# A recommendation tower on one core: gathered rows copied aside by ScalarE, GpSimd's gathers split in two, and edits at the two ends

## The reference

```python
x = stack([tbl_f[ids[:, f]] for f in range(32)], axis=1)             # 1024 x 32 x 32
h = x
for i, (W, b) in enumerate([(W0, b0), (W1, b1), (W2, b2)]):          # 128, 128, 1 outputs
    z = einsum('bhd,bmd,ohm->bod', h, x, W.reshape(O, H, 32))
    z = relu(z + b)
    h, direct = (z[:, :half], z[:, half:]) if i < 2 else (None, z)   # half = 64
    directs.append(direct)
feat = concat([sum(concat(directs, 1), -1), dense_ctx], 1)           # 1024 x 145
y = relu(relu(feat @ W_top1 + b_top1) @ W_top2 + b_top2) @ W_top3    # 1024 x 1
```

## Time and profile before

| what | value |
|---|---|
| time, median of 3 runs | 1219.24 us (1217.71 to 1222.34) |
| profiled execution: time, span | 1219.3 us, 1217.3 us |
| busy: PE, DVE | 1120.3 us (92%), 1055.8 us (87%) |
| busy: POOL, ACT | 717.5 us (59%), 579.5 us (48%) |
| chain that ended last, by engine | DVE 36%, issue 23%, POOL 21%, PE 12%, DMA 5% |
| mean granted TensorE clock | 0.983 |
| transfers | 154.95 MB, mean 127 GB/s |

### The profile page before, as it was taken

How to read it: one execution, slowest core, us unless ns; L and a number is a source line. 1 busy time by engine, 2 the same in 40 slices (tenths; PEclk the granted TensorE clock), 3 DMA queues, 4 the chain that set the end, 5 groups by cost and what they waited for, 6 DMA issues and landing times.

```text
span 1217.3 us, 11479 instructions
## 1 busy us (share of the span) xinstructions
PE 1120.3 (92%) x3736; PEld 682.4 (56%) x3736; DVE 1055.8 (87%) x573; ACT 579.5 (48%) x477; POOL 717.5 (59%) x333
## 2 busy tenths in 40 slices
PE   0699989999999999999999999899999999999998
PEld 0356655655555555565565656556565555656655
DVE  1689987998898989899898989889899898999973
ACT  0344554554555445455444545545445554544534
POOL 6277665667766666766566686656676665663110
PEclk9899998999999999999999999999999999999999
DMA  7555553455454435555344555434554543354200
GB/s 231 175 156 156 130 137 105 117 134 155 136 146 107 137 94 155 141 143 148 107 128 109 155 138 145 134 103 119 136 155 129 148 125 110 112 152 126 54 1 0
DMA packets 63414, 154.95 MB, mean 127 GB/s; under 512 B 12753, under 2 KB 29394, under 8 KB 63394
## 3 DMA queue, kind: packets, MB, share of 16 engines
q1 hardware_dynamic: 52594, 147.05, 42.2%
q0 software_dynamic: 8192, 4.21, 2.4%
q10 hardware_dynamic: 2608, 3.44, 0.9%
HBM read 95.79 MB, written 8.39 MB: 86 GB/s over the span
## 4 chain that ended last, share of the span: by engine, by line
DVE 36%; issue 23%; POOL 21%; PE 12%; DMA 5%; SPq 1%; DVEq 1%; ACT 0%; POOLq 0%; ACTq 0%
POOL gathered L330 15%; DVE prod L476 12%; DVE raw L531 11%; PE z_ps L635 11%; DVE prod_lo L537 7%; POOL prod_lo L350 6%; DMA x_roll<-x_dram 3%; DVE raw L502 3%; DVE top_a L551 1%; DVE lo L509 1%; DVE h2x L544 1%; PE mlp_ps L635 1%; POOL prod_lo L341 1%; DMA x_base<-x_dram 1%; DMA gathered<-in_table,rows_sb 0%
## 5 line engine op out<-in xcount | busy, mean ns | idle before, releaser
L635 PE MATMUL z_ps<-prod,w_sb 128*128 128x512 f32 x1280 | 582.0, 599 | 49.9 <-DVE prod L489 27.5
L330 POOL DMA_INDIRECT gathered<-in_table,rows_sb x256 | 431.8, 1687 | 96.3 <-issue 72.2
L531 DVE TENSOR_TENSOR raw<-h_roll,x_roll 128x2048 f32<-128x2048 f32 x160 | 363.1, 2285 | 81.5 <-POOL prod_lo L350 80.2
L872 ACT CAST prod_hi<-raw 128x2048 fp32r<-128x2048 f32 x160 | 304.9, 1906 | 257.6 <-DVE raw L531 253.0
L635 PEld LDWEIGHTS z_ps<-prod,w_sb 128*128 128x128 f32 x1280 | 244.1, 192 | 318.5 <-issue 306.3
L341 POOL TENSOR_TENSOR prod_lo<-raw,prod_hi 128x2048 fp32r<-128x2048 f32 x32 | 146.7, 4585 | 335.4 <-DVE prod_lo L537 290.2
L476 DVE TENSOR_TENSOR prod<-mlp_ps,x_roll 128x2048 f32<-128x2048 f32 x124 | 281.0, 2284 | 17.1 <-DMA x_roll<-x_dram 6.8
L635 PE MATMUL z_ps<-prod_hi,w_hi 128*128 128x512 f32 x648 | 245.3, 459 | 43.5 <-POOL prod_lo L350 41.4
L537 DVE TENSOR_TENSOR prod_lo<-raw,prod_hi 128x2048 fp32r<-128x2048 f32 x98 | 223.6, 2283 | 0.0
L635 PE MATMUL z_ps<-prod_lo,w_hi 128*128 128x512 f32 x648 | 209.3, 404 | 0.0
L635 PE MATMUL z_ps<-prod_hi,w_lo 128*128 128x512 f32 x648 | 209.1, 403 | 0.0
(11 more groups left out here) (61 smaller groups left out, 371.6 us busy)
## 6 DMA issues: line engine op xcount, KB each, us to landing
x_roll<-x_dram SPq DMA_DIRECT2D x128, 512.0 KB, 4.8
x_base<-x_dram SPq DMA_DIRECT2D x32, 512.0 KB, 3.6
h_roll<-h_roll SPq DMA_DIRECT2D x32, 448.0 KB, 4.5
h_roll<-h_roll SPq DMA_DIRECT2D x32, 384.0 KB, 5.4
h_roll<-h_roll SPq DMA_DIRECT2D x32, 320.0 KB, 6.0
x_dram<-gathered SPq DMA_DIRECT2D x64, 128.0 KB, 1.7
h_roll<-h_roll SPq DMA_DIRECT2D x32, 192.0 KB, 7.2
gathered<-in_table,rows_sb POOLq DMA_INDIRECT x256
```

The lines of the kernel that those rows point to most:

```text
L330: nc.gpsimd.indirect_dma_start(gathered[:, u, g * DIM:(g + 1) * DIM], None, table, bass.IndirectOffsetOnAxis(ap=rows_sb[:, col:col + 1], a ...
L531: nc.vector.tensor_tensor(raw[:, RAW_SLOT[r], :, :], hs, xs, ALU.mult).then_inc(raw_ready, 1)
L635: return nc.tensor.matmul(*args, **kw)
L872: nc.scalar.copy(prod_hi[:, SPLIT_SLOT[r], :, :], raw[:, RAW_SLOT[r], :, :]).then_inc(hi_ready, 1)
```

## The change

1. **A copy aside.** ScalarE copies the gathered chunk c+1 into a new buffer `x_late` (2 buffers, 128x256) in step c, between the roundings of A1 and B2 (`copy_late`). `h2x` reads `x_late` in place of `gathered`. The gathers of chunk c+3 now wait for that copy of chunk c-1 (`late_copied`), which ran two steps earlier, and not for h2x.
2. **Gathers four and four.** GpSimd's order becomes lo3, (rows for the next four chunks where u is 1), four gathers, lo1, four gathers.
3. **Late load of an MLP weight.** `wt2_sb` has no buffer of its own: it lies in a part of `x_roll`, and is loaded by SyncE after the last roll of h, not at the start by ScalarE's queue. The room pays for `x_late`.
4. **Start.** TensorE runs 6 extra matmuls (128x512, float32) once x of chunk 0 is stored, and 3 after layer 0 of chunk 0; what they write to `z1_ps` is never read. SyncE loads `x_base` of chunk 1 before `x_part16` and the second half of `x_roll` of that chunk (it waits, as before, for the first two products), not behind them.
5. **Last chunk.** Its layer 1 accumulates in `z0_ps`, so it need not wait until ScalarE has drained `z1_ps` of chunk 30; TensorE runs `layer2_u` of chunk 30 after B0, not ahead of it. The MLP's banks are taken in the order z1, mlp, z0, with other waits to match.

The diff, cut to its core:

```diff
+        x_late = sb("x_late", [P, 2, PART])
...
+        wt2_sb = x_roll[:, 0, M2, :].rearrange("p (k n) -> p k n", n=TOP2)
...
-        mlp_banks = [t[:, k * BANK:(k + 1) * BANK] for t in (z0_ps, mlp_ps, z1_ps) for k in range(2)]
+        mlp_banks = [t[:, k * BANK:(k + 1) * BANK] for t in (z1_ps, mlp_ps, z0_ps) for k in range(2)]
+
+        def z1_of(c):
+
+            return z0_ps if is_last(c) else z1_ps
...
-                wait(pool, h2x_ready, freed)
-                for g in range(GATHERS):
+                wait(pool, late_copied, freed)
+                for g in range(part * GATHERS // 2, (part + 1) * GATHERS // 2):
...
-                lo1(c)
                 ahead = UNROLL - 1
-                if not isinstance(c, int) or c + ahead < CHUNKS:
+                more = not isinstance(c, int) or c + ahead < CHUNKS
+                if more:
                     if u == 1:
                         make_rows(group + 1)
-                    gather(c + ahead, (u + ahead) % UNROLL, group if u == 0 else group + 1)
+                    gather(c + ahead, (u + ahead) % UNROLL, group if u == 0 else group + 1, 0)
+                lo1(c)
+                if more:
+                    gather(c + ahead, (u + ahead) % UNROLL, group if u == 0 else group + 1, 1)
...
                     if b == 1:
+                        if isinstance(c, int) and c == 1:
+                            sp.wait_ge(prod_ready, PAIRS0)
+                            load_base(c)
...
-                if isinstance(c, int) and c == 1:
-                    sp.wait_ge(prod_ready, PAIRS0)
-                    load_base(c)
...
             roll_h(CHUNKS - 1, (CHUNKS - 1) % 2)
+            sp.wait_ge(raw_ready, (CHUNKS - 1) * SPLIT1)
+            sp.dma_start(wt2_sb, wt2).then_inc(mlp_loaded, 16)
...
                 dve.wait_ge(u_done, c + 1)
+                dve.wait_ge(late_copied, c + 1)
                 wait(dve, z2_done, group)
-                nc.vector.tensor_tensor(h2x[:, u, :], u_ps[:, :], gathered[:, u, :], ALU.mult).then_inc(h2x_ready, 1)
+                nc.vector.tensor_tensor(h2x[:, u, :], u_ps[:, :], x_late[:, u % 2, :], ALU.mult).then_inc(h2x_ready, 1)
...
+            def keep_clock(count):
+
+                for _ in range(count):
+                    mm(z1_ps[:, 0:BANK], w0_sb[:, 0, :], w0_sb[:, :, :].rearrange("p r n -> p (r n)"),
+                       start=True, stop=True)
 
             pe.wait_ge(w0_ready, 1)
+            pe.wait_ge(x_stored[0], 32)
+            keep_clock(6)
             for k in range(PAIRS0):
                 layer0(0, 0, k)
             pe.wait_ge(w16_ready, 1)
             layer0_pairs16(0)
+            keep_clock(3)
...
+            def copy_late(c, u, group):
+
+                act.wait_ge(gather_done[u], (group + 1) * (16 * GATHERS))
+                wait(act, h2x_ready, c - 1)
+                nc.scalar.copy(x_late[:, u % 2, :], gathered[:, u, :]).then_inc(late_copied, 1)
...
                 round_products(c, A1)
+                if not is_last(c):
+                    copy_late(c + 1, (u + 1) % UNROLL, group if u < UNROLL - 1 else group + 1)
                 round_products(c, B2)
```

More of the change, by code:

```diff
@@ L244, in build_tower @@
         lo1_ready = sem("lo1_ready")
+        late_copied = sem("late_copied")
         h0_copied = sem("h0_copied")
@@ L319, in make_rows, with gather @@
                                         ALU.add).then_inc(rows_made, 1)
-            def gather(c, u, group):
+            def gather(c, u, group, part):
                 made = settled(pool, group + 1)
@@ L358, in step @@
                     lo3(c - 1)
-                lo1(c)
                 ahead = UNROLL - 1
-                if not isinstance(c, int) or c + ahead < CHUNKS:
+                more = not isinstance(c, int) or c + ahead < CHUNKS
+                if more:
                     if u == 1:
                         make_rows(group + 1)
-                    gather(c + ahead, (u + ahead) % UNROLL, group if u == 0 else group + 1)
+                    gather(c + ahead, (u + ahead) % UNROLL, group if u == 0 else group + 1, 0)
+                lo1(c)
+                if more:
+                    gather(c + ahead, (u + ahead) % UNROLL, group if u == 0 else group + 1, 1)
             make_rows(0)
             for c in range(UNROLL - 1):
-                gather(c, c, 0)
+                for part in range(2):
+                    gather(c, c, 0, part)
             over_chunks(pool, step)
@@ L616, in _ @@
             dve.wait_ge(split_used, CHUNKS * SPLIT1)
-            nc.vector.tensor_copy(wt2_hi, wt2_sb[:, :, :]).then_inc(wt2_hi_ready, 1)
+            nc.vector.tensor_copy(wt2_hi, wt2_sb).then_inc(wt2_hi_ready, 1)
             dve.wait_ge(wt2_hi_ready, 1)
-            nc.vector.tensor_tensor(wt2_lo, wt2_sb[:, :, :], wt2_hi, ALU.subtract).then_inc(wt2_ready, 1)
+            nc.vector.tensor_tensor(wt2_lo, wt2_sb, wt2_hi, ALU.subtract).then_inc(wt2_ready, 1)
             for n in range(BATCH_HALVES * M1):
@@ L677, in layer1 @@
             def layer1(c, u, k):
-                whole(z1_ps, first1(c) + k, slot1(c, u) + k, w1_sb[:, k * PAIR:(k + 1) * PAIR, :], start=k == 0)
+                whole(z1_of(c), first1(c) + k, slot1(c, u) + k, w1_sb[:, k * PAIR:(k + 1) * PAIR, :], start=k == 0)
             def layer0_pairs16(c):
@@ L716, in step @@
                     layer0(*after, 1)
-                wait(pe, h2_ready, 2 * c)
-                wait(pe, direct1_ready, c)
+                if is_last(c):
+                    pe.wait_ge(h1_ready, 2 * CHUNKS)
+                    pe.wait_ge(direct0_ready, CHUNKS)
+                else:
+                    wait(pe, h2_ready, 2 * c)
+                    wait(pe, direct1_ready, c)
                 layer1(c, u, 0)
@@ L722, in step @@
                     layer0_pairs16(c + 1)
-                if not_first(c):
+                    if not_first(c):
+                        layer2_u(c - 1, (u - 1) % UNROLL)
+                split(z1_of(c), c, B0)
+                if is_last(c):
                     layer2_u(c - 1, (u - 1) % UNROLL)
-                split(z1_ps, c, B0)
                 layer1(c, u, 1)
-                split(z1_ps, c, B1)
+                split(z1_of(c), c, B1)
                 layer1(c, u, 2)
-                split(z1_ps, c, A1)
+                split(z1_of(c), c, A1)
                 if u == 0 and not_first(c):
                     layer2_sum(c, group - 1)
-                split(z1_ps, c, B2)
+                split(z1_of(c), c, B2)
                 if not pool_makes_lo3(c):
-                    split(z1_ps, c, B3, stop=True)
+                    split(z1_of(c), c, B3, stop=True)
+            def keep_clock(count):
+                for _ in range(count):
+                    mm(z1_ps[:, 0:BANK], w0_sb[:, 0, :], w0_sb[:, :, :].rearrange("p r n -> p (r n)"),
+                       start=True, stop=True)
             pe.wait_ge(w0_ready, 1)
+            pe.wait_ge(x_stored[0], 32)
+            keep_clock(6)
             for k in range(PAIRS0):
@@ L765, in _ @@
             pe.wait_ge(mlp_loaded, 16 * 7)
-            pe.wait_ge(direct0_ready, CHUNKS)
-            pe.wait_ge(h1_ready, 2 * CHUNKS)
+            pe.wait_ge(direct1_ready, CHUNKS - 1)
+            pe.wait_ge(h2_ready, 2 * (CHUNKS - 1))
+            pe.wait_ge(prod_ready, first1(CHUNKS - 1) + WHOLE1)
             pe.wait_ge(direct_summed, CHUNKS // BATCH_HALVES)
@@ L827, in _ @@
             act.dma_start(wt1b_sb[:, :], wt1b).then_inc(mlp_loaded, 16)
-            act.dma_start(wt2_sb[:, :, :], wt2).then_inc(mlp_loaded, 16)
             act.dma_start(wt3_sb[:, :], wt3).then_inc(mlp_loaded, 16)
@@ L855, in relu1 @@
                     nc.scalar.activation(h2[half * HID:(half + 1) * HID, s, :],
-                                         z1_ps[0:HID, half * BANK:(half + 1) * BANK], ACT.Relu,
+                                         z1_of(c)[0:HID, half * BANK:(half + 1) * BANK], ACT.Relu,
                                          bias=b1_sb[0:HID, :]).then_inc(h2_ready, 1)
-                nc.scalar.activation(direct[HID:P, s, :], z1_ps[HID:P, :], ACT.Relu,
+                nc.scalar.activation(direct[HID:P, s, :], z1_of(c)[HID:P, :], ACT.Relu,
                                      bias=b1_sb[HID:P, :]).then_inc(direct1_ready, 1)
@@ L920, in _ @@
             copy_h0(0, 0)
+            copy_late(0, 0, 0)
             over_chunks(act, step)
```

1 line of the change is left out of this document (removed).

## The result

| | before | after |
|---|---|---|
| median (range, runs) | 1218.47 us (1216.57 to 1222.34, 4) | 1134.82 us (1133.59 to 1136.96, 4) |
| ratio, 95% interval | | 0.9312 [0.9284, 0.9339] |
| profiled execution: time, span | 1219.3, 1217.3 us | 1133.59, 1131.7 us |
| PE, DVE busy | 92%, 87% | 97%, 90% |
| mean granted TensorE clock | 0.983 | 0.999 |

The account below looks back on a forecast made before the run. The prediction took VectorE's losses to late lo3 as the bound, TensorE being next. From 1219.3 us it took 68.3 (steady chunks), 3 (start) and 3 (last chunk), giving 1145 us; 8-in-10 range 1134 to 1180.

Parts of the forecast that it names:

- The bound: Steady chunks: VectorE loses time to late lo3, behind eight gathers; with lo3 on time TensorE bounds at 33.15 us a chunk.
- Where 123 us of VectorE's loss would go: Steady chunks: VectorE's 80.2 us waiting for lo3 and 43 us of stretched raw16 go; only the part above TensorE's pace returns.
- Lateness of lo1: Steady chunks: four gathers ahead of lo1 delay it; 0.25 us a chunk beyond VectorE's slack, making 33.4 us a chunk.
- the sign "idle ahead of lo1 falls under 2 us": GpSimd in steady chunks: lo1's idle time ahead of it was to fall from 9.5 us to under 2.
- The start: Start: earlier x_base load taken as 2 us, extra matmuls as 1; 3 us saved, from 0 to 6.
- The last chunk: Last chunk: first layer-1 product starts without the drain wait, at full clock; 3 us saved, from 1 to 5.
- The copy at nothing: ScalarE, each chunk: one copy of 0.40 us taken to cost 0; 11 us if wholly on the path.
- the late weight at nothing: Late load of wt2, some 35 us before it is needed: taken to cost 0.
- The inference of the Trainium skill: Gather descriptor writing not held up by a tensor_tensor; if so, lo1 never late and 33.15 us a chunk, 7 us less.
- (a): Steady chunks: VectorE stays the bound, gathers missing seams in most chunks; 1169 to 1210 us, middle 1178; chance 0.22.
- (b): Every steady chunk: lo1 3.8 us late into A1, lo3 2.1 us into raw16; 1264 us; chance 0.03.
- (c): Steady chunks: lo3 as late as before, its four gathers missing as often as eight; 1213 to 1219 us; chance 0.05.

Follow-up runs that it names:

- x9: Changed kernel, TensorE leaving out the rounded part times the weights' remainder in two of five split products (A1, B2); 1083.19 us, 0.8875 of the kernel before.
- x10: Changed kernel, TensorE leaving out the rounded part times the weights' remainder in four of five split products (B0, B1, A1, B2); 1083.34 us.
- x2: Only the edits at start and last chunk and the late load of wt2; gathers and h2x as in the kernel before; 1208.95 us, 0.9917 of it.
- x3: Changed kernel with the copy aside, but GpSimd's order as before (lo3, lo1, eight gathers); 1207.42 us, 0.9922 of the kernel before.
- x12: Changed kernel, rounded part times weights' remainder left out in B0, B1, A1, B2, and GpSimd's order as before (lo3, lo1, eight gathers); 1196.75 us.
- x1: Changed kernel with start and last chunk put back as before; copy aside, gathers four and four and late wt2 load kept; 1142.74 us, 0.9372.
- x8: Changed kernel with the last chunk put back as before; 1138.19 us, 0.9347 of the kernel before.
- x11: Changed kernel with ScalarE's copy aside made five times over in each chunk; 1135.65 us, 0.9303 of the kernel before.
- x5: Changed kernel with all eight gathers ahead of lo1 and none behind it; 1180.30 us, 0.9695 of the kernel before.

## Why the prediction was right

**The bound.** Right. The views led to lo3 late behind eight gathers, and to 33.0 us of TensorE as what lies under it. The floor of 33.15 us was read from one chunk without gathers, with 0.15 added for the sum of layer 2, and the mean chunk came out at 33.15; a hit to 0.01 us is partly luck, as the one chunk with the sum is 0.78 us longer than its neighbour.

**Where 123 us of VectorE's loss would go.** Right: 75 came back, the rest turned into VectorE's slack. x9 shows it by going on to 31.35 us when TensorE gets less to do.

**Lateness of lo1 (0.25 us a chunk, 7.0 us in all).** Mis-sized: it was nothing. The prediction gave the four gathers 8.8 us, or 13.4 with a miss, in a window of 9.5 us between lo3 and the end of rest B0. In the 27 steady chunks they were done 6.8 to 9.8 us after lo3, no gather missed two seams, and the window was 10.4 us on average, since VectorE now waits for TensorE inside it (0.81 us in the chunk shown). lo1 then also waits for ScalarE's rounding of B1 (130.0 us in the waits), but that is the small part: it started 0.6 to 0.8 us after rest B0, against 0.2 in most chunks of x10. So it stood idle for 1.9 to 4.3 us, and the sign "idle ahead of lo1 falls under 2 us" was wrong. Where VectorE is the bound (x10) the gathers do hold lo1 up in 5 of 27 chunks, by 0.9 us, which is free.

**The start (3 us).** It measured 6.9, and the term that failed is one that the sum left at nothing. Up to the first pair the edits gave 3.7 us (60.07 to 56.37), close to the 3 of the prediction. Its parts are near too: x_base's wait went from 6.31 to 3.33, then 1.70 for x_roll, so that the second product came 1.9 us earlier (2 were taken), and the granted clock stayed at 1.00 (1 was taken for it). The other 3.2 us lie between the first pair and the h2x of chunk 0: that step took 38.72 us before and 35.52 after. It is a chunk like the others, in which lo3 was late behind eight gathers, and the sum counted only the 28 chunks behind it. All four kernels with eight gathers behind lo1 need 38.6 to 39.7 us there (before, x2, x3, x12), the ten others 35.3 to 37.9; x1, which has none of the start's edits, needs 36.17. The recorded text of x1, written after the result, has this as "the second step, where lo3 was late too".

**The last chunk (3 us).** Right: 3.3, with x8 for its parts.

**The sum.** The misses all went to the same side: 7.1 us for lateness, 3.9 at the start, 0.3 at the end, 11.3 in all. That they did not cancel is why the time lies at the bottom of the range.

**The copy at nothing, the late weight at nothing.** Right for the copy (x11). The late load was never tried alone; x1, which has it, leaves no room for a cost in the steady part.

**Rivals.** (a) and (b) rest on a late lo1; x5 shows that the mechanism exists and its price (3.3 us in the pair), four gathers just don't reach it. (c) needed the last four gathers to miss seams as often as eight did; lo3 waits for VectorE in all 30 chunks.

**The inference of the Trainium skill.** The Trainium skill (SBUF — State Buffer, "Who interferes with whom") infers that writing descriptors is not held up by a tensor_tensor. For these gathers that stays refuted: one took 1.88 us beside products with both inputs in SBUF (574.09), and 0.95 us where it started beside the pair that reads mlp_ps (613.34 in x5; the pair runs from 609.64 to 614.11). By that inference the prediction reckoned 33.15 us a chunk, 7 us less than its forecast, and that is where the chunk came out; but the number was met because four stretched gathers still fit ahead of lo1, not because they weren't stretched.

## What to carry to other kernels

Look into durations as well as waits: raw16 took 0.4 us in some places and 3.3 in another, where lo3 ran beside it, and no wait showed the loss. An in-order queue that mixes long background work with short urgent work can be cut at the places where the urgent work idles anyway, and here the buffer that ties the background work to a late reader had to be freed first; each half alone gave nothing or cost 11%. How much goes ahead matters as well: four gathers cost nothing that can be seen, eight 1.6 us a chunk. Before sizing what a removed wait gives back, find a stretch in the same trace that already runs without it: here it gave the next bound to 0.2 us. And count that wait in every place where it occurs, the first step too.

## What the runs showed of the hardware that was not expected

A gather that misses two seams between VectorE's instructions (6.49 us, 16 times before) did not occur once in the changed kernel; all 256 gathers, min, median and max ns:

```profile
L336 POOL DMA_INDIRECT gathered<-in_table,rows_sb x256: 941/1888/3055, 4.4 to 991.1; - x128
```

Such gathers occur only in the kernels with all eight gathers behind lo1 (16 in the kernel before and in x2, 14 in x3, 12 in x12, up to 7.14 us long), and in none of the ten others, not even in x5 with eight in a row ahead of lo1.

In the row of 6.49 us the gather started 1.0 us after the start of the pair A1, B2; in the changed kernel the second gather behind lo1 starts within 0.1 us of that pair (556.62 against 556.65). That distance alone does not decide it. In the kernel before 20 gathers started 1.00 to 1.05 us after that pair: all sixteen long ones, and four of 2.05 to 2.09 us, such as this one, with its pair at 602.44:

```profile
603.46 2.08 POOL L330 DMA_INDIRECT gathered<-in_table,rows_sb  x1 [0.31 <-issue]
```

And in x3 thirteen gathers of 7.12 to 7.14 us started only 0.36 to 0.38 us after it. What decides it stays open.
